# A fused Mamba block and int8 layer: the conv taps, the softplus and two bank uses reordered inside a 16-slot program

## The reference

```python
x = x + mamba(layernorm(x)); x = x + int8_matmul(layernorm(x), rhs)
# mamba, 1024 inner channels, 16 states, chunks of 128 rows:
xi, z = split(x @ in_proj_w.T)
xc = silu(causal_conv_4_taps(xi) + conv_b)
xp = xc @ x_proj_w.T
delta = softplus(xp[..., 0:1] * dt_w[:, 0] + dt_b)      # Bp, Cp: the other 32 columns of xp
A_bar = exp(delta * A);  BX = delta * Bp * xc
A_cum = exp(min(cumsum(log(max(A_bar, 1e-10))), 80))
wcum = cumsum(BX / max(A_cum_shifted, 1e-10))
h = A_cum * wcum / max(A_bar, 1e-10) + h_before * A_cum   # per state, carried from chunk to chunk
y = (sum over states of Cp * h + D_param * xc) * silu(z);  out = y @ out_proj_w.T
```

## Time and profile before

| what | value |
|---|---|
| median of three runs | 6191.47 us (6191.06 to 6192.29) |
| span of the profiled execution, first to last instruction | 6189.9 us |
| PE matmul busy | 5686.4 us, 92% |
| DVE busy | 5633.4 us, 91% |
| ACT busy | 3734.6 us, 60% |
| POOL busy | 2744.1 us, 44% |
| mean granted TensorE clock | 0.989 |

### The profile page before, as it was taken

One profiled execution on the slowest core, in us unless ns is written; L12 is line 12 of the kernel. 1 busy time (PEld: TensorE's weight loads), 2 busy tenths in 40 slices (PEclk: granted clock), 3 DMA queues, 4 the chain that ended last, 5 costly groups with the idle time before them and its releaser, 6 DMA issues.

```text
span 6189.9 us, 77161 instructions
## 1 busy us (share of the span) xinstructions
PE 5686.4 (92%) x16152; PEld 2632.6 (43%) x16152; DVE 5633.4 (91%) x7057; ACT 3734.6 (60%) x4618; POOL 2744.1 (44%) x2138
## 2 busy tenths in 40 slices
PE   5999999999999999999999999999999999999997
PEld 2444444444444444444444444444444444444443
DVE  4999999999999999999999999999999999999997
ACT  3666665665666666656666666566566666665664
POOL 2444444444444444444444444444444444444443
PEclk9999999999999999999999999999999999999998
DMA  1121121121111211211212112112121121121120
GB/s 64 11 17 19 14 17 15 14 19 13 16 18 14 17 16 14 19 15 14 19 13 17 16 14 19 15 14 19 13 16 18 14 17 15 14 19 15 14 17 11
DMA packets 157893, 104.23 MB, mean 17 GB/s; under 512 B 121008, under 2 KB 121008, under 8 KB 157488
## 3 DMA queue, kind: packets, MB, share of 16 engines
q1 hardware_dynamic: 157488, 100.71, 17.8%
HBM read 42.63 MB, written 16.78 MB: 10 GB/s over the span
## 4 chain that ended last, share of the span: by engine, by line
PE 37%; DVE 31%; issue 20%; ACT 3%; DVEq 2%; ACTq 0%; DMA 0%; SPq 0%
PE state L971 13%; DVE acc L1321 11%; PE cum L961 10%; DVE term L1311 6%; PE fbank L866 5%; DVE conv L1167 4%; DVE conv L1159 2%; PE ebank L936 2%; PE ebank L916 2%; PE fbank L879 2%; DVE xn L1277 1%; ACT xiT L568 1%; DVE dx L1222 1%; DVE delta L1213 1%; PE fbank L850 1%
## 5 line engine op out<-in xcount | busy, mean ns | idle before, releaser
L699 ACT ACTIVATE decay<-cum,neg_a 128x1024 f32<-128x1024 f32 x1024 | 1138.6, 1112 | 1944.8 <-PE cum L961 1942.4
L971 PE MATMUL state<-sources,tri_upto 128*128 128x512 f32 x4096 | 1980.6, 606 | 187.4 <-DVE term L1311 187.1
L473 POOL TENSOR_SCALAR room<-total,limit 128x1024 f32<-128x1024 f32 x1024 | 1352.8, 1321 | 1653.9 <-ACT cum L704 1448.2
L463 POOL TENSOR_SCALAR step<-delta,limit 128x1024 f32<-128x1024 f32 x1024 | 1243.4, 1214 | 1661.2 <-PE cum L961 1038.5
L961 PE MATMUL cum<-step,tri_before 128*128 128x512 f32 x4096 | 1940.7, 596 | 3.5 <-DVE sources L1298 3.5
L1311 DVE SCALAR_TENSOR_TENSOR term<-state,crow,decay 128x1024 f32<-128x1024 f32 x1024 | 1308.8, 1278 | 247.4 <-PE state L971 135.9
L1321 DVE TENSOR_TENSOR acc<-acc,term 128x1024 f32<-128x1024 f32 x1024 | 1459.2, 1425 | 0.2
L1298 DVE SCALAR_TENSOR_TENSOR sources<-cum,brow,dx 128x1024 f32<-128x1024 f32 x1024 | 1303.1, 1273 | 12.1 <-ACT cum L704 12.1
L971 PEld LDWEIGHTS state<-sources,tri_upto 128*128 128x128 f32 x4096 | 744.5, 191 | 1068.5 <-issue 941.7
L961 PEld LDWEIGHTS cum<-step,tri_before 128*128 128x128 f32 x4096 | 777.7, 192 | 941.7 <-issue 935.6
L704 ACT ACTIVATE cum<-room,pos_a 128x1024 f32<-128x1024 f32 x1024 | 1143.6, 1117 | 17.6 <-POOL room L473 2.7
(11 more groups left out here) (125 smaller groups left out, 3972.7 us busy)
## 6 DMA issues: line engine op xcount, KB each, us to landing
hfirst<-hrows SPq DMA_DIRECT2D x496, 64.0 KB, 3.9
xt<-in_x SPq DMA_DIRECT2D x64, 256.0 KB, 2.6
hrows<-term SPq DMA_DIRECT2D x1024, 4.0 KB, 1.7
xres<-in_x SPq DMA_DIRECT2D x64, 256.0 KB, 2.7
out_x<-xres SPq DMA_DIRECT2D x64, 256.0 KB, 2.1
gate_last<-gate SPq DMA_DIRECT2D x512, 0.5 KB, 2.1
win<-in_w_in SPq DMA_DIRECT2D x2, 2048.0 KB, 10.7
hrows<-hrows SPq DMA_DIRECT2D x64, 64.0 KB, 2.3
```

The lines of the kernel that those rows point to most:

```text
L463: nc.gpsimd.tensor_scalar(step[s % 2][:, :], delta[t.parity][:, :], limit[:, s:s + 1], 0.0, ALU.min, ALU.max).then_inc(step_ready, 1)
L473: nc.gpsimd.tensor_scalar(room[:, :], total[:, :], limit[:, s:s + 1], 0.0, ALU.min, ALU.max).then_inc(room_ready, 1)
L699: nc.scalar.activation(decay[s % 4][:, :], cum[s % 2][:, :], ACT.Exp, scale=neg_a[:, s:s + 1]).then_inc(decay_ready, 1)
L971: last = nc.tensor.matmul(state[:, cols], tri_upto[:, :], source[s % 2][:, cols], start=True, stop=True)
```

## The change

No arithmetic is added or removed and every operation stays on its engine. The programs are written in another order:

- The taps 0 to 2 on DVE go by halves of the channels (`front_tap(t, tap, h)`, 4 blocks each). Taps 0a and 1a stand in slot 4, 2a and 0b in slot 5, 1b and 2b with `halo_out` in slot 6; before, whole taps stood in slots 5, 6 and 7. `norm_moments` goes from slot 4 to 7.
- ACT's `silu` with its two table loads goes from slot 8 to 7, the copy of `proj` from 9 to 8, `abs` to the end of slot 9; `exp` stands ahead of the decay of slot 10, `over` behind it; the copies of xc0 and xc1 move one slot up; `square` goes ahead of the decay of slot 11, `ln` behind it. The join on DVE gets a wait of its own for `ln`. `decay_once` goes from slot 14 to the head of 15, `norm_guess` from 5 to 8.
- On PE `front_proj` goes from slot 9 to 8, the xc transposes to slots 9 and 10, part 1 of the output projection from 8 to 9, and `total1` ahead of `states` of slot 13.
- `total1` and the transposes of `xn` use the bank `ebank` in place of `fbank`.
- A table `ROOM_POOL` would allow `room` on ACT for some slots. It lists all 16, so every one stays on POOL.

```diff
-FRONT_ACT = ("xi0", "xi1", "xiT0", "tap3a", "xiT1", "tap3b", "z0", "xcT", "proj", "abs", "exp", "over", "xc0",
-             "ln", "xc1", "square", "z1", "total0", "total1", "ct")
+FRONT_ACT = ("xi0", "xi1", "xiT0", "tap3a", "xiT1", "tap3b", "z0", "xcT", "proj", "xc0", "abs", "exp", "over", "xc1",
+             "square", "ln", "z1", "total0", "total1", "ct")
...
+ROOM_POOL = (0, 1, 2, 3, 4, 5, 6, 7, 8, 9, 10, 11, 12, 13, 14, 15)
...
             def front_total(t, h):
+                earlier = t.shift(-2)
                 pe.wait_ge(front_dve, at(FRONT_DVE, t, "delta"))
-                front_free(t, f"total{h}")
-                nc.tensor.matmul(fbank[:, :], tri_before[:, :], delta[t.parity][:, h * HALF:(h + 1) * HALF],
+                if h == 0:
+                    front_free(t, "total0")
+                elif earlier is not None:
+                    pe.wait_ge(end_dve, at(END_DVE, earlier, "x2"))
+                nc.tensor.matmul((fbank, ebank)[h][:, :], tri_before[:, :], delta[t.parity][:, h * HALF:(h + 1) * HALF],
...
-            def front_tap0(t):
...
+            def front_tap(t, tap, h):
+                half = "ab"[h]
+                dve.wait_ge(front_act, at(FRONT_ACT, t, f"tap3{half}"))
+                dve.wait_ge(front_dve, at(FRONT_DVE, t, f"tap{tap - 1}{half}" if tap > 0 else "halo_in"))
+                for k in range(4 * h, 4 * h + 4):
...
+                dve.wait_ge(front_act, at(FRONT_ACT, t, "ln"))
                 nc.vector.scalar_tensor_tensor(out=dt_y[:, :], in0=dt_over, scalar=ln_join, in1=dt_y[:, :], op0=ALU.subtract,
```

More of the change, by code:

```diff
@@ L90, in slot_at, with room_at @@
     return tile.n * NS + slot + 1
+def room_at(tile, slot):
+    same = [s for s in range(NS) if (s in ROOM_POOL) == (slot in ROOM_POOL)]
+    return tile.n * len(same) + same.index(slot) + 1
 def ring_at(tile, slot):
@@ L522, in body @@
                         limit_step(nxt, s + 3 - NS)
-                    if s + 2 < NS:
+                    if s + 2 < NS and s + 2 in ROOM_POOL:
                         limit_sum(t, s + 2)
-                    elif more:
+                    if more and s + 2 >= NS and s + 2 - NS in ROOM_POOL:
                         limit_sum(nxt, s + 2 - NS)
@@ L699, in decays, with rooms @@
                 nc.scalar.activation(decay[s % 4][:, :], cum[s % 2][:, :], ACT.Exp, scale=neg_a[:, s:s + 1]).then_inc(decay_ready, 1)
+            def rooms(t, s):
+                if s == min(x for x in range(NS) if x not in ROOM_POOL):
+                    act.wait_ge(front_act, at(FRONT_ACT, t, "total1"))
+                user, old = before(t, s, 1)
+                if user is not None:
+                    act.wait_ge(growth_ready, slot_at(user, old))
+                nc.scalar.activation(room[:, :], total[:, :], ACT.Relu, bias=ln_top, scale=neg_a[:, s:s + 1]).then_inc(room_ready, 1)
             def growths(t, s):
                 act.wait_ge(decay_ready, slot_at(t, s))
-                act.wait_ge(room_ready, slot_at(t, s))
-                nc.scalar.activation(cum[s % 2][:, :], room[:, :], ACT.Exp, scale=pos_a[:, s:s + 1]).then_inc(growth_ready, 1)
+                if s in ROOM_POOL:
+                    act.wait_ge(limited, room_at(t, s))
+                    nc.scalar.activation(cum[s % 2][:, :], room[:, :], ACT.Exp, scale=pos_a[:, s:s + 1]).then_inc(growth_ready, 1)
+                else:
+                    act.wait_ge(room_ready, room_at(t, s))
+                    nc.scalar.activation(cum[s % 2][:, :], room[:, :], ACT.Exp, bias=ln_top, scale=-1.0).then_inc(growth_ready, 1)
             def finish(t):
@@ L741, in start @@
                 for s in range(2):
+                    if s not in ROOM_POOL:
+                        rooms(t, s)
                     decays(t, s)
@@ L751, in body @@
                         end_q(prev2)
-                    if s == 10 and more:
-                        front_abs(nxt)
+                    if more:
+                        if s == 10:
+                            front_exp(nxt)
+                        if s == 11:
+                            front_square(nxt)
+                        if s == 15:
+                            decay_once(nxt)
                     if more or s + 2 < NS:
+                        if slot not in ROOM_POOL:
+                            rooms(ahead, slot)
                         decays(ahead, slot)
@@ L783, in body @@
                         end_qT(prev2)
[L784 removed]
+                    if more2 and s == 8:
                         norm_guess(t.shift(2))
@@ L1346, in start @@
                 front_halo(t)
-                front_tap0(t)
-                front_tap(t, 1)
-                front_tap(t, 2)
+                for h in range(2):
+                    for tap in range(3):
+                        front_tap(t, tap, h)
+                front_halo_out(t)
                 front_rows(t)
```

127 lines of the change are left out of this document (66 added, 61 removed).

## The result

The changed kernel takes 6110.55 us (median of 4 runs, 6095.47 to 6111.31), against 6191.88 us (6191.06 to 6193.03) for the kernel before on the same chip. The ratio is 0.9864, with a 95% interval of 0.985 to 0.9877. It is faster by 81 us where 157 were forecast. That lies in the stated range, 4 us from its upper end, and in the interval that the prediction gave to rival 1 (6090 to 6150), not in the forecast's own (5990 to 6090). The profiled execution has a span of 6108.9 us.

The account below looks back on a forecast made before the run. PE, ACT and DVE waiting on each other was taken to cost the time; 3.7 - 1.2 = 2.5 us a tile over 63 tiles, 157 us, gave 6034.5 us, range of 8 in 10 5980 to 6115.

Parts of the forecast that it names:

- rival 1: Slots 4 to 6: POOL meets the taps, two more disturbed groups cost 1.6 us a tile, time 6135 us; chance 0.14.
- the knot: Around slot 11: PE waits for ACT, ACT for PE, DVE for both; poly's wait for square, 131.4 us, should near zero.
- ACT's margins: Slots 9 to 12: ACT's results come before PE or DVE wants them, shortest margin 0.7 us, others 1.4 to 2.1.
- D(7) to D(12): From DVE's term opening slot 7 to that opening slot 12: PE-bound, 30.48 to 26.8 us, gain 3.7 a tile.
- 14 blocks of 1.72 us: PE's work from states of slot 7 up to states of slot 11, with two xc transposes of 0.49: 25.06 us.
- Slots 4 to 6: DVE's work counts in full: tap 2 in (2.18), norm_moments out (1.26), two tap waits (0.24); 1.2 us longer a tile.
- the two waits between taps: Taps 1a and 2b stand directly behind 0a and 1b, whose results they need: 0.12 us each, 0.24 together.
- the disturbance: POOL's instructions lengthening tap groups, 2.17 to 2.96 us: taken as unchanged, bounds 0.79 us less to 1.6 us more.
- Slots 12 to 15: Rest of the tile, including total1 in the other bank: no gain taken, 0.
- The skip product: POOL's 2.36 us instruction holding up an add of DVE: may slip clear, 0 to 0.8 us gain, taken as 0.
- Rival 4: Join waits for ln behind slot 13's decay, which waits for PE's cum: 3.7 us lost, 6267 us; chance 0.08.

Follow-up runs that it names:

- Run 1: Kernel before with only ACT's new order in slot 11 (xc1 copy and square ahead of the decay, ln behind): 6111.33 us, ratio 0.9857.
- run 6: Kernel before with only the taps by halves in slots 4 to 6, norm_moments in slot 7, norm_guess in slot 8: 6395.82 us, ratio 1.0327.
- run 2: Changed kernel plus one unread 128x512 filler matmul on PE in slot 7: 6036.73 us, ratio 0.9752.
- Run 4: Changed kernel with room of slots 6, 7 and 8 on ACT and not on POOL: 6008.69 us, ratio 0.9699.
- run 3: Changed kernel with part 1 of the previous tile's output projection moved from slot 9 to slot 7, ahead of state: 5989.12 us, ratio 0.9672.
- run 7: The kernel of run 3 with the eight taps of slot 4 ahead of add and not behind it: 5946.56 us, ratio 0.96.
- run 5: Changed kernel with the edits of run 3 and run 4 together: 5898.83 us, ratio 0.9527.
- run 8: The kernel of run 5 plus four unread 128x256 filler matmuls on PE in slot 0, behind the transposes of q: 5965.19 us, ratio 0.9636.

## Why the prediction came out as it did

**The bound and the knot: right.** `poly` no longer waits for `square`, the join follows, and PE's waits for the copies are nearly gone (the z1 row from 109.4 to 5.2 us, the xc row from 68.6 to 1.4). ACT's margins held: DVE's waits for `acc` and `over` come to 1.2 and 3.7 us in the whole run of the kernel after. Run 1 shows that ACT's order does it, run 6 that the taps don't.

**D(7) to D(12): the size was off by 1.1 us.** The term was 30.48 to 26.8. The means are 30.48 and 27.91, and 26.99 in run 2, where the clock doesn't fall. What failed is the term of 14 blocks of 1.72 us (25.06 us), which takes every block at the full clock. The condition beside it, "if PE never waits in it", came true: behind `states` of slot 7, which starts 1.42 us after D(7) and was put at 1.41, PE doesn't wait up to slot 12. But in 33 of 61 tiles these first blocks run at 1.2 GHz, and the stretch takes 28.70 us and not 26.99. I had counted PE's wait of 0.94 us ahead of `states` of slot 7 as slack that costs nothing. In the kernel after it is 1.96 us in every tile, mostly because slot 6 just before it takes 7.34 us and not 6.63. Run 4 shortens slot 4 but not slot 6, and keeps the wait (2.07 us) and the low stretches; runs 2 and 3 cut it to 1.10 and 0.24 us, and no low stretch begins in slot 7. It cost 0.92 us a tile. It is the same wait that the prediction used to say that slots 4 to 6 count on DVE alone.

**Slots 4 to 6: the size was off by 1.2 us.** The term was +1.2; the mean is +2.43. Tap 2, the moments and the two waits between taps come to about what was worked out: run 4, which has one disturbed tap a tile like the kernel before, is longer than it by 1.13. What was mis-sized is the disturbance, taken as 0 within bounds of -0.79 to +1.6: it is 1.3, near the upper bound. Rows showed one group of three disturbed; now two of three are, and the first by two instructions of POOL. Two more long taps a tile are 1.57 us, the upper bound; the `add` of slot 6 pays 0.57 more (1.78 and not 1.21), and a small instruction of the last tile's end in the same slot (`ygT`) pays 0.80 less (0.15 and not 0.95). This is rival 1, whose price of 1.6 a tile and time of 6135 us were near; I gave it 0.14, and should have placed POOL's `room` and `step` against the new starts of the taps instead of keeping the old count. The rule of the Trainium skill that was weighed there ("SBUF — State Buffer", "Who interferes with whom") agrees with runs 4 and 7: without POOL's `room` in its way the first group takes 2.31 us and not 3.84, and taken ahead of it 2.61, while the next group then meets it and takes 3.75 and not 2.18. What the rule alone does not give is which of the two engines pays in a chain of short instructions: in the kernel before `room` cut in 0.29 us behind the start of a group, while `step`, at 2987.52 in the midst of another, which ran from 2986.46 to 2988.63, had to wait and took 2.10 us.

**Slots 12 to 15: a gain of 1.17 that I had taken as 0.** The skip product is the part of it that was foreseen, up to 0.8. The timeline of POOL and of DVE in the kernel after:

```profile
3077.82 2.35 POOL L462 TENSOR_TENSOR acc<-xiT,dskip 128x1024 f32<-128x1024 f32 x1
```

```profile
3078.03 1.28 DVE L1356 SCALAR_TENSOR_TENSOR term<-state,crow,decay 128x1024 f32<-128x1024 f32 x1
3079.23 1.28 DVE L1343 SCALAR_TENSOR_TENSOR sources<-cum,brow,dx 128x1024 f32<-128x1024 f32 x1
3080.42 1.22 DVE L1366 TENSOR_TENSOR acc<-acc,term 128x1024 f32<-128x1024 f32 x1
```

The product ends at 3080.17, ahead of `add` of slot 14, which takes 1.22 us and not 2.03. Slot 14 is shorter by 0.83 us in the mean. In runs 1 and 6, which keep the old banks for the totals, it isn't. That the two banks do it fits, but no run changed them alone, so it is not shown. The other 0.33 us lie in slot 15; their cause I did not follow.

**The sum.** 3.7 - 1.2 = 2.5 was forecast. Measured: 2.57 - 2.43 + 1.17 - 0.14 = 1.17. Two losses, 0.92 by the clock and 1.3 by POOL, and one gain that was put at its lower bound. Runs 3, 4 and 5 take the two losses away nearly independently, but they share a root: the slot 6 that POOL and the taps make longer is the one behind which PE waits. That the time still lies in the stated range is in part luck: without the gain of 1.17 in slots 12 to 15 it would have been about 6184 us (an estimate, 6110.6 + 63 x 1.17). Of the causes of the shortfall the rivals had one, POOL at the taps; the clock was in none. Rival 4 (`ln` too late) didn't come: the join waits nowhere in the kernel after. In run 1 a wait for `over` of 34.8 us is left, which the new order of PE in the kernel after doesn't have. Slot 11 itself is longer there by 1.31 us than in the kernel after (8.35 against 7.04).

**Left open.** Why slot 15 is shorter; where the 3.2 us a tile come from that runs 1 and 6 together do not have; what of run 8's 1.08 us a tile is the filler's own time and what is its delay of the copy of q; and why the clock falls after PE's idle time in some tiles and not in others (in the kernel after the wait of 1.96 us stands in every tile, and a low stretch begins behind it in 33 of 61).

## What to carry to other kernels

An idle stretch of the engine that bounds the next stretch isn't free slack: look at the granted clock right behind it, and where it falls put useful work into the gap (run 3, 121 us), a filler only where the gap is there in nearly every round (run 2 won 74 us, run 8 lost 66). Where only some rounds pay, sort them by the granted clock: their two lengths give the price at once (28.70 and 26.99 us here). Short two-input instructions of DVE that are moved meet other instructions of GpSimd than before: lay both timelines over each other at the new starts, and take the other engine's instruction out of the stretch (run 4) before you shift the group (run 7). Time the parts of a change one by one: here one part is worth 80 us by itself, another costs 203, and the whole gives 81, so much of its worth lies in what was not timed alone.

## What the runs showed of the hardware that I had not expected

A wait of TensorE of 1.96 us in a kernel in which it is busy 93% was followed by four matmuls at a granted clock of 0.54 (3.58 us and not 1.96), but only in 33 of 61 tiles with the same wait. With the wait cut to 1.10 us by a filler the next four took 1.96 us, and 14 stretches at the 1.2 GHz level were left of 59. Adding matmuls made the kernel 74 us faster.

A group of eight tap instructions (2.18 us) took 3.05 us with one instruction of GpSimd inside and 3.84 us with two: each time a single tap took 1.11 us and not 0.34. GpSimd's own cost was small there: `room` took 1.11 us and `step` 1.24 in the middle of such a group of 3.84 us at 3117.84. In other places it was GpSimd that took 2.14 us for the same `room` (3084.82).
